# A routed FFN, a mixer and a routed FFN again on one core: transposes by VectorE's 32x32 squares, quadrants exchanged through HBM, and stationary weights in the router and the mixer's output

## What is computed

```python
x = x + 0.5 * ffn(layernorm(x))
x = x + mixer(layernorm(x))
x = x + 0.5 * ffn(layernorm(x))

# ffn, T tokens, 32 experts of 64 hidden units, and a shared one of 128:
scores = sigmoid(tokens @ router_weight.T)            # [T, 32]
# groups of 8 experts; the best 2 groups; of these the best 4 experts; weights sum to 2.5
expert_out = (silu(gate(t)) * up(t)) @ down           # of the chosen experts, weighted
out = sum of the four + shared expert

# mixer: projection to gate and value, a convolution of width 5 along the sequence,
# a linear recurrence h = tanh(a) * h + u, an output projection, residual and a layer norm
```

## Time and profile before

| | |
|---|---|
| median of three runs | 674.26 us (672.54 to 674.37) |
| profiled execution | 674.34 us |
| span in its profile, first to last instruction | 672.5 us |
| TensorE busy | 656.8 us, 98% of the span |
| VectorE busy | 550.6 us, 82% |
| GpSimd busy | 444.9 us, 66% |
| ScalarE busy | 419.4 us, 62% |

### The profile page before, as it was taken

The page is one execution under the profiler, slowest core; times in us unless marked ns, Lnnn a source line. Parts: engine busy times, 40 slices in busy tenths (PEclk is TensorE's granted clock), DMA queues, the critical chain, the costliest instruction groups (busy, mean ns, idle before and its releaser), DMA issues. The chain is left out here.

```text
span 672.5 us, 9867 instructions
## 1 busy us (share of the span) xinstructions
PE 656.8 (98%) x3048; PEld 530.6 (79%) x3048; DVE 550.6 (82%) x1545; ACT 419.4 (62%) x800; POOL 444.9 (66%) x444
## 2 busy tenths in 40 slices
PE   7899999999999999999999999999999999999997
PEld 6687888888888887888888888888878778777785
DVE  5888889988978888889779798688989967967765
ACT  3656576675576656766567765767576576655554
POOL 1256558775676776766767766868676777676654
PEclk9899999999999999999999999999999999999999
DMA  8100100100001000010001000000000000100001
GB/s 215 53 17 20 32 0 21 33 20 17 4 18 32 20 17 21 1 44 9 16 21 31 21 1 24 13 17 20 17 9 13 1 20 3 34 1 17 20 1 31
DMA packets 24853, 15.55 MB, mean 23 GB/s; under 512 B 6592, under 2 KB 21856, under 8 KB 24800
## 3 DMA queue, kind: packets, MB, share of 16 engines
q1 hardware_dynamic: 24224, 14.90, 7.7%
q10 hardware_dynamic: 576, 0.02, 0.1%
HBM read 11.83 MB, written 3.08 MB: 22 GB/s over the span
## 5 line engine op out<-in xcount | busy, mean ns | idle before, releaser
L564 POOL TENSOR_TENSOR hid_lo<-hid,hid_hi 128x512 fp32r<-128x512 f32 x270 | 348.6, 1295 | 192.3 <-ACT hid_hi L671 191.9
L820 DVE TENSOR_TENSOR weighted<-gate_ps,wb 128x512 f32<-128x512 f32 x256 | 175.1, 684 | 68.6 <-ACT gate_ps L663 63.6
L663 ACT ACTIVATE gate_ps<-gate_ps 128x512 f32<-128x512 f32 x256 | 148.7, 581 | 122.4 <-PE gate_ps L1109 119.3
L671 ACT ACTIVATE hid_hi<-hid 128x512 fp32r<-128x512 f32 x272 | 170.5, 627 | 61.0 <-DVE hid L833 56.6
L833 DVE TENSOR_TENSOR hid<-weighted,up_ps 128x512 f32<-128x512 f32 x256 | 174.4, 681 | 8.4 <-POOL hid_lo L564 0.5
L1177 PE MATMUL down_ps<-hid_lo,wt_hi 128*128 128x512 f32 x272 | 107.9, 397 | 0.2 <-DVE hid_lo L841 0.2
L1174 PE MATMUL down_ps<-hid_hi,wt_hi 128*128 128x512 f32 x272 | 107.7, 396 | 0.0
L1175 PE MATMUL down_ps<-hid_hi,wt_lo 128*128 128x512 f32 x272 | 107.5, 395 | 0.0
L1107 PE MATMUL gate_ps<-xT_hi,wt_hi 128*128 128x512 f32 x170 | 71.9, 423 | 0.0
L1107 PE MATMUL up_ps<-xT_hi,wt_hi 128*128 128x512 f32 x170 | 68.4, 402 | 2.3 <-DVE hid L833 2.3
L1108 PE MATMUL gate_ps<-xT_lo,wt_hi 128*128 128x512 f32 x170 | 67.4, 397 | 0.0
(11 more groups left out here) (194 smaller groups left out, 1104.0 us busy)
## 6 DMA issues: line engine op xcount, KB each, us to landing
wb<-wT_hbm SPq DMA_DIRECT2D x60, 64.0 KB, 2.1
x_ln<-in_L_attn_x SPq DMA_DIRECT2D x8, 256.0 KB, 3.1
x_res<-in_L_attn_x SPq DMA_DIRECT2D x8, 256.0 KB, 2.8
out_x<-x SPq DMA_DIRECT2D x7, 256.0 KB, 2.3
raw_gate<-in_L_ffn_gate_w SPq DMA_DIRECT2D x4, 256.0 KB, 4.7
raw_up<-in_L_ffn_up_w SPq DMA_DIRECT2D x4, 256.0 KB, 5.0
raw_down<-in_L_ffn_down_w SPq DMA_DIRECT2D x4, 256.0 KB, 5.2
wT_hbm<-wT SPq DMA_DIRECT2D x15, 64.0 KB, 1.5
```

The lines of the kernel that those rows point to most:

```text
L564: nc.gpsimd.tensor_tensor(hid_lo[s][:, :], hid[s][:, :], hid_hi[s][:, :].bitcast(F32), ALU.subtract)\
L663: nc.scalar.activation(bank[:, :] if j else silu_sb[:, :], bank[:, :], ACT.Silu).then_inc(silu_done, 1)
L671: nc.scalar.activation(hid_hi[s][:, :], hid[s][:, :], ACT.Copy).then_inc(hid_hi_done, 1)
L820: V.tensor_tensor(weighted[j % 2][:, :], gate_ps[n % BANKS][:, :], wb[u % 2][:, :], ALU.mult)\
```

## The change

VectorE can transpose a tile by squares of 32x32: within each square rows and columns are exchanged, and the squares stay where they are. The change uses this in place of TensorE's transposes for some blocks. Such a `shuffle` step writes the squares of a 128x512 tile to SBUF; SP stores the result to HBM (a scratch tensor) and, when the store has landed, loads it again in four DMAs, one for each quadrant of 32 partitions, so that the quadrants come to stand where a full transpose has them. The store is issued in the slot of the shuffle, the loads one slot later. Blocks 2 to 7 of norm 1, 2 to 5 of norm 2, 1 to 4 of norm 4, 1 to 6 of the first FFN's output and 1 to 4 of the mixer's output go this way; the other blocks, and the last FFN's output, stay with TensorE. The memory for it is that of the raw weights, which are no longer needed by then.

In these blocks the tokens of a block come out in another order (quadrants first), and the copies that leave PSUM put them back by strided access. The rest `xT_lo` of a moved norm and the two sums behind a moved FFN or mixer output are done by GpSimd from SBUF ("low", "sum ffn 1", "sum mixer"), where VectorE did them from PSUM.

The router of blocks 2 to 7 (first FFN) and 1 to 6 (last FFN) now has the weights as stationary operand, four copies of the 32 experts side by side, and three matmuls of 128x512. ScalarE copies one quadrant of partitions for each 128 tokens out of the result (`spread_logits`, four copies of 32x128), and VectorE turns these squares into the PSUM bank `routed`. The mixer's output of blocks 1 to 4 has stationary weights too. The routing weights of all but the first unit are turned by VectorE's squares, and the store and the four loads of `wb` give them their order; five of these broadcasts have runs of 32 elements (`w_tiles_hbm`), the others of 128. The router's weights are loaded four times at the start. Lastly the step behind `gsum` gets a second copy of `gsum` in PSUM (`gsum_too`), so that its two inputs no longer both lie in SBUF. The tables of slots are written anew, and SP goes through the slots like the other engines.

```diff
+MOVED_NORM = {1: range(2, NBLK), 2: range(2, NBLK - 2), 4: range(1, 5)}
+MOVED_FFN = range(1, NBLK - 1)
+MOVED_MIX = range(1, 5)
+SPREAD = {1: range(2, NBLK), 4: range(1, NBLK - 1)}
...
+        def from_quadrants(t, n):
+            return t.rearrange("(a c) (b n) -> b c a n", a=QUADS, b=QUADS)[n]
+
+        def to_quadrant(t, n):
+            return t[QUAD * n:QUAD * n + QUAD, :].rearrange("c (a n) -> c a n", a=QUADS)
...
-        PREPARE = {"transpose 1": 0, "xT high 1": 1, "xT low 1": 1, "router 1": 2, "silu logits 1": 3,
-                   "route 1": even(2, 12), "weights 1": 13}
+        PREPARE = {"xT high 1": 0, "low 1": 0, "router 1": 2, "spread logits 1": 2, "shuffle logits 1": 3,
+                   "silu logits 1": 5, "route 1": even(4, 14), "weights 1": 14.5}
...
+            def store_norm(k, b):
+                sp.wait_ge(x_shuffled[k], b - MOVED_NORM[k][0] + 1)
+                sp.dma_start(x_hbm[k], shuffled_x[k]).then_inc(x_stored[k], 16)
+
+            def move_norm(k, b):
+                sp.wait_ge(x_stored[k], (b - MOVED_NORM[k][0] + 1) * 16)
+                sp.wait_ge(xT_lo_done[k], b)
+                for n in range(QUADS):
+                    sp.dma_start(to_quadrant(moved_x[k], n), from_quadrants(x_hbm[k], n)).then_inc(x_moved[k], 16)
...
-            sp.wait_ge(dve_const, 1)
-            sp.dma_start(raw[0:E, WROUTER, :], router_w).then_inc(raw_loaded[0], 16)
+            for n in range(SPLIT):
+                sp.dma_start(raw[E * n:E * n + E, WROUTER, :], router_w).then_inc(raw_loaded[0], 16)
...
+            def xT_low_moved(k, b):
+                pool.wait_ge(xT_hi_done[k], b + 1)
+                nc.gpsimd.tensor_tensor(lo_of(k, b), moved_x[k], hi_of(k, b).bitcast(F32), ALU.subtract)\
+                  .then_inc(xT_lo_done[k], 1)
...
+            def spread_logits(k, b):
+
+                act.wait_ge(logits_made[k], b - SPREAD[k][0] + 1)
+                act.wait_ge(logits_ready[k], b)
+                for n in range(QUADS):
+                    rows = slice(QUAD * n, QUAD * n + QUAD)
+                    dst, src = spread[k][rows, :], side[rows, P * n:P * n + P]
+                    if b not in MOVED_NORM[k]:
+                        dst, src = dst.rearrange("e (t r) -> e t r", t=TT), in_tiles(side[rows, :])[:, :, n, :]
+                    last = nc.scalar.activation(dst, src, ACT.Copy)
+                last.then_inc(logits_spread[k], 1)
...
+            def shuffle_norm(k, b):
+                n = b - MOVED_NORM[k][0]
+                dve.wait_ge(ln_normed[k], b + 1)
+                if n > 0:
+                    dve.wait_ge(x_moved[k], n * MOVE)
+                V.transpose(shuffled_x[k].rearrange("p (b t r) -> p t b r", b=QUADS, t=TT),
+                            by_dim(normed[k][:, :, :])).then_inc(x_shuffled[k], 1)
...
+            def shuffle_weights(k, b):
+                dve.wait_ge(route[k], b * ROUTE + ROUTE)
+                V.transpose(wS[k], w_tok[:, :, :].rearrange("p t e -> p (t e)")).then_inc(w_shuffled[k], 1)
...
+                    V.tensor_tensor(gsum_too.rearrange("p t g -> p (t g)"), best1[:, :], best2[:, :], ALU.add)
                     st.done(V.tensor_tensor(gsum[:, :, :].rearrange("p t g -> p (t g)"), best1[:, :], best2[:, :],
                                             ALU.add))
...
+                if b in SPREAD[k]:
+                    product(side[:, :], wt_hi[:, WROUTER, :], hi_of(k, b), lo_of(k, b), wt_lo[:, WROUTER, :],
+                            True, True).then_inc(logits_made[k], 1)
+                    return
...
-            def transpose_route(k, b):
-                pe.wait_ge(route[k], b * ROUTE + ROUTE)
-                nc.tensor.transpose(side[:, 0:P], w_tok[:, :, :].rearrange("p e t -> p (e t)"), ident[:, :])\
-                  .then_inc(route_transposed[k], 1)
-
```

369 lines of the change are left out of this document (261 added, 108 removed), and 3 rows, old and new, of the table END.

## The result

The changed kernel takes 694.72 us (median of four runs, 694.04 to 695.27), the kernel before 674.32 beside it. The ratio is 1.031, with an interval of 1.029 to 1.032: slower by 3%, where 656 us and faster was forecast. The profiled execution took 694.04 us, its span is 692.2.

A forecast was written before the change was run, and what follows sets the result against it. TensorE was taken as the bound: 674.34 - 20.6 (its work) - 1.4 (its waits) + 2.5 (ScalarE) + 0.5 (weight loads) + 1.0 (start) = 656 us. Range 650 to 661, chance 0.65.

The forecast's parts named there:

- TensorE is the bound in every stage but the start and the end: Whole kernel: TensorE 98% busy, so its 20.6 us less work and 1.4 us fewer waits come off the time.
- TensorE's prices: TensorE costs from differences of starts, such as 0.234 us per 128x512 matmul; a block falls from 79.30 to about 75.4.
- the step on ScalarE: Spread copies behind the router in slot 2 of k=4 units, `normed` groups after: 0.5 us per block, 2.5 in all.
- the prediction's own sign of being wrong: Prediction is wrong if ScalarE's row of small copies holds up every unit; also if a square exceeds 2 us, a move 9.
- Hidden: GpSimd's five more 128x512 operations per block, 62.5 of 75.4 us, cost no time: `hid_lo` is read three slots later.
- The rule weighed in the prediction: Trainium skill: full 128x128 transposes belong on TensorE; its 311 ns would make 1.24 us for 512 columns on VectorE.
- A move: Store to HBM plus four loads on SP: 6.2 us against a 7.0 us deadline, so nothing was counted.
- The start: Router weights loaded four times, so TensorE waits longer at the start: +1.0 us (0.7 to 1.4).
- The term of 0.5 us for the weights in runs of 32 elements: Five routing-weight broadcasts in short pieces, loads already late in the last unit: 0.5 us (0 to 3.1).
- Late moves: Rival: HBM moves take 9 to 10 us, costing TensorE 10 us, total time 661 to 670 us; chance 0.20.
- VectorE the bound by dear squares: Rival: squares cost per column like the reciprocal, VectorE needs 86 us per block, total time 709 us; chance 0.10.
- the gain is eaten by units that wait on each other: Rival: units waiting on each other cancel the saving, total time within 2 us of 674; chance 0.05.

The follow-up runs named there:

- the best version: Changed kernel with only slots moved: norms in the second, third and middle units, then four more places; 661.78 us, ratio 0.982.
- after_router_twice: Changed kernel with each of the twelve stationary-weight routers issued twice, 8.4 us more TensorE work; 694.86 us, ratio 1.031.
- eased slots: Changed kernel, same operations, with slots moved in the second and third unit and the middle k=4 and k=1 units; 669.46 us, ratio 0.993.
- k4_norms_2_3: Changed kernel with normalise 3 in slot 1 instead of 3 and norm 2 in slot 2 instead of 3, middle k=4 units; 685.89 us.
- k4_slots: Changed kernel with normalise 3, norm 2, its move and xT earlier and normalise 4 later in middle k=4 units; 683.64 us.

## Why the prediction was wrong

*Wrong: "TensorE is the bound in every stage but the start and the end", and what is taken from it comes off the time.* The condition that the prediction put behind it, "as long as nobody else is late", failed. TensorE's prices hold: its work for a block comes to the 75.5 us above, where they gave 75.4, and the k=1 units of the best version, in which TensorE waits for nobody, run at that pace. But in the middle units of the changed kernel itself TensorE's work is worth nothing (`after_router_twice`).

*Wrong: the step on ScalarE.* It named the right place, slots 2 to 4 of a k=4 unit with the spread and two groups of `normed`, and took 0.5 us per block, 2.1 at most. The spread itself costs about that much when doubled with eased slots (0.42 per group, 0.62 in a k=4 unit). The row as a whole was taken too small: without `normed` of norm 3 in it, and with norm 2 a slot earlier, a k=4 unit is 1.65 us shorter (`k4_norms_2_3`), within the step's bounds but three times its figure. So the prediction's own sign of being wrong, a row on ScalarE that holds up every unit, came in part: the small copies with the two groups behind them, not the copies alone. What the step left out is the norms: that `normed` waits for `shift`, and that a norm stands one slot or none ahead of its application. It read the order at that place only, and neither slot 10 of a k=4 unit, slot 1 of a k=1 unit nor the second and third unit. The k=4 units came out 4.0 us above TensorE's work in them (41.80 against 37.8), the k=1 units 2.0 (39.73 against 37.74): some 22 us in seven units, where the step had 2.5 in the whole run. The second and third unit alone cost 11.5 more than before, of which moving slots alone gave 10.0 back.

*Wrong: "Hidden" for GpSimd.* Its work came out as counted (62.15 us for 62.5), but the reason given was that `hid_lo` is read three slots later. The results of GpSimd with a near reader are the four steps of `shift` and the new `xT_lo`, for which TensorE waited 5.0 us. At two of the places shown (slot 10 of the k=4 unit, slot 1 of the k=1 unit) 128x512 operations of 1.30 us that are new on GpSimd stand ahead of `shift`; what these cost in the changed kernel was not tested by itself (in the kernel before such operations raised the wait, and hardly the time).

*Right, and without weight for the result:* a square of 128x512 took 0.69 to 0.71 us (forecast 0.69), one of 128x128 0.30 to 0.32 (0.28); `gdiff` 222 ns in the median (199 to 229) as forecast, down from 610; VectorE's block 66.0 us (forecast 68). By form, xcount, busy us, mean ns:

```profile
L1052 DVE STREAM_TRANSPOSE raw_gate<-normed 128x512 f32<-128x512 f32 x14 | 9.9, 704 | 0.0
...
L1080 DVE STREAM_TRANSPOSE raw_down<-w_tok 128x128 f32<-128x128 f32 x15 | 4.5, 301 | 0.0
...
L1076 DVE STREAM_TRANSPOSE routed<-raw_down 128x128 f32<-128x128 f32 x12 | 3.8, 316 | 0.1
...
L1061 DVE STREAM_TRANSPOSE raw_gate<-ffn_sb 128x512 f32<-128x512 f32 x5 | 3.4, 686 | 0.0
...
L1071 DVE STREAM_TRANSPOSE raw_down<-side 128x512 f32<-128x512 f32 x4 | 2.8, 710 | 0.0
```

```profile
L1132 DVE TENSOR_TENSOR routed<-gsum,routed x16: 199/222/229, 18.4 to 640.8; 128x64 f32<-128x64 f32 x16
```

The rule weighed in the prediction, that a full transpose belongs on TensorE ("VectorE: DVE Perf Modes" of the Trainium skill, sections "The three transpose paths" and "Rules for kernel authors"), would have given the right sign, but not by the mechanism that the prediction joined to it, dear squares. Its figure for 128x128, 311 ns, agrees with the 301 to 316 here, but four times that is too dear for 512 columns: 0.70 us, not the estimate of 1.24. And with eased slots the change is faster.

A move took 5.8 us (store issued at 298.77, the four loads issued by 300.80 + 1.73 = 302.53, 2.0 to land; forecast 6.2), and `xT_hi` waited for none. SP's queue (start, time to issue), then stores, loads and weights by the page (xcount, KB each, us to landing):

```profile
298.77 0.34 SPq L572 DMA_DIRECT2D x_hbm<-raw_gate  x1
300.80 1.73 SPq L578 DMA_DIRECT2D raw_up<-x_hbm  x4
```

```profile
x_hbm<-raw_gate SPq DMA_DIRECT2D x14, 256.0 KB, 2.0
raw_up<-x_hbm SPq DMA_DIRECT2D x56, 64.0 KB, 2.0
wb<-w_hbm SPq DMA_DIRECT2D x40, 64.0 KB, 2.2
...
wb<-w_tiles_hbm SPq DMA_DIRECT2D x20, 64.0 KB, 2.4
```

The start: TensorE's wait for the router's weights grew from 0.59 us to 1.36, 0.8 for the forecast 1.0:

```profile
6.24 1.12 PE L1376 MATMUL gate_ps<-ident,raw 128*128 128x128 f32 x4 [1.36 <-DMA raw<-in_L_ffn_router_weight]
```

The term of 0.5 us for the weights in runs of 32 elements was not seen: these loads landed in 2.4 us against 2.2, and none of TensorE's waits names them.

*The rivals.* Late moves: false (`k4_slots`). VectorE the bound by dear squares: false in its price; it gave the sign with 0.10. That the gain is eaten by units that wait on each other had 0.05, and only as "no change": this was the true mechanism, and it took more than the gain.

## What to carry to other kernels

A table of slots is part of a change's cost: for each step that another engine waits for, count the slots between maker and reader, and what now stands ahead of the maker in its queue; a reader in an in-order engine that waits holds up all that is behind it. A busy share of 98% tells which engine is last now, not how far behind the next chain is: here the chain through ScalarE, VectorE and GpSimd, with the new work in the new slots, took 81.5 us for a block, more than TensorE's 79.3 had been. When a change that removes work from the bound comes out slower, try its operations with other slots before giving it up: the same operations ran at 694.7 and at 661.8 us.
